# Attention mixing and a 16-expert feed-forward layer on one core: keys later, each expert's down projection at the end of its own slot, one shared chunk in halves

## The reference, cut to what matters

```python
xn = layernorm(x)                                   # x: 2 x 1024 tokens of 256
# attention part (a linear form, no softmax)
Xn = layernorm(xn, gamma, beta)
Q, K, V = split(Xn @ W_in + b_in, 3)
K, V = rotary(K), rotary(V)
A = sum over tokens of unit(K) * unit(V)            # one row of 256 per batch
A = 0.5 * A + 0.5
attn = (A[:, None, :] * Q) @ W_out + b_out + xn
# feed-forward part
scores = softmax(xn @ gate_w.T);  topk of 4 out of 16 experts, weights renormalised
for each expert e, at most 128 tokens (in order):
    y[tokens] += (silu(xg @ w_gate[e]) * (xg @ w_up[e])) @ w_down[e] * weight
shared = (silu(xn @ sw_gate) * (xn @ sw_up)) @ sw_down      # inner width 352
out = x + attn + y + shared
```

## Time and profile before

| | |
|---|---|
| median of 3 runs | 172.38 us (170.6 to 172.52) |
| the profiled execution | 171.0 us, span 169.2 us |
| TensorE busy | 152.4 us, 90% of the span |
| VectorE, ScalarE, GpSimd busy | 64%, 44%, 58% |
| mean granted TensorE clock | 0.983 |

### The profile page before, as it was taken

How to read it: one execution, slowest core, us unless ns; L and a number is a source line. 1 busy time by engine, 2 the same in 40 slices (tenths; PEclk the granted TensorE clock), 3 DMA queues, 4 the chain that set the end, 5 groups by cost and what they waited for, 6 DMA issues and landing times.

```text
span 169.2 us, 3124 instructions
## 1 busy us (share of the span) xinstructions
PE 152.4 (90%) x1005; PEld 134.3 (79%) x1005; DVE 108.7 (64%) x317; ACT 74.6 (44%) x227; POOL 98.1 (58%) x127
## 2 busy tenths in 40 slices
PE   7987797999998999999989999999899999999450
PEld 5556676999886889988779988978898987999340
DVE  1887998587863387799695769638942225920680
ACT  3034437676467984557483543633422354100000
POOL 8675699782237318897653995576523333306930
PEclk9999999999999999999999999999999999999967
DMA  5999969691014657486557487593832222378067
GB/s 151 344 369 338 568 223 346 202 284 28 2 16 114 196 150 187 133 198 140 153 108 188 133 192 142 126 205 128 190 37 31 35 31 31 31 215 280 5 236 260
DMA packets 25507, 28.53 MB, mean 169 GB/s; under 512 B 4114, under 2 KB 24563, under 8 KB 25460
## 3 DMA queue, kind: packets, MB, share of 16 engines
q1 hardware_dynamic: 21042, 22.90, 43.1%
q0 software_dynamic: 3072, 4.33, 15.5%
q10 hardware_dynamic: 1378, 1.12, 2.1%
HBM read 21.64 MB, written 8.79 MB: 180 GB/s over the span
## 4 chain that ended last, share of the span: by engine, by line
DMA 38%; issue 16%; POOL 15%; DVE 13%; PE 11%; ACT 2%; POOLq 1%; DVEq 1%; SPq 0%
DMA ysum<-eo,idx 32%; POOL xg L426 6%; POOL ysum L434 3%; DMA x_all<-ysum 3%; PE bank L247 3%; DVE st L671 3%; POOL xn_all L465 3%; PE bank L249 2%; PE bank L248 2%; DMA x_all<-in_x 2%; DVE xn_all L980 1%; POOL wqt L416 1%; DMA rows<-wd 1%; DVE xt_all L701 1%; DVE mv L674 1%
## 5 line engine op out<-in xcount | busy, mean ns | idle before, releaser
L434 POOL DMA_INDIRECT ysum<-eo,idx x16 | 31.6, 1975 | 33.4 <-DMA ysum<-eo,idx 22.2
L247 PE MATMUL bank<-wkvr_s,xt_all 128*128 128x256 f32 (+1 forms) x96 | 29.9, 311 | 6.9 <-DVE xt_all L701 3.7
L248 PE MATMUL bank<-wkvr_s,xt_all 128*128 128x256 f32 (+1 forms) x96 | 27.7, 288 | 0.0
L249 PE MATMUL bank<-wkvr_s,xt_all 128*128 128x256 f32 (+1 forms) x96 | 27.6, 288 | 0.0
L247 PEld LDWEIGHTS bank<-wkvr_s,xt_all 128*128 128x128 f32 x96 | 18.6, 194 | 8.5 <-DVE xt_all L701 4.7
L1173 PE MATMUL bank<-xgt,wgu 128*128 128x128 f32 (+1 forms) x192 | 24.0, 275 | 0.0
L1173 PEld LDWEIGHTS bank<-xgt,wgu 128*128 128x128 f32 (+1 forms) x192 | 22.4, 187 | 0.1
L426 POOL DMA_INDIRECT xg<-rows,idx x16 | 17.3, 1084 | 8.4 <-issue 4.0
L247 PE MATMUL bank<-xt_all,sw_s 128*128 128x512 f32 (+1 forms) x48 | 21.0, 438 | 0.0
L248 PE MATMUL bank<-xt_all,sw_s 128*128 128x512 f32 (+1 forms) x48 | 18.9, 394 | 0.0
L249 PE MATMUL bank<-xt_all,sw_s 128*128 128x512 f32 (+1 forms) x48 | 18.9, 393 | 0.0
(11 more groups left out here) (167 smaller groups left out, 352.5 us busy)
## 6 DMA issues: line engine op xcount, KB each, us to landing
wgu<-in_w_gu SPq DMA_DIRECT2D x16, 368.0 KB
rows<-xn_all SPq DMA_DIRECT2D x4, 512.0 KB, 6.8
wdn<-in_w_dn SPq DMA_DIRECT2D x16, 128.0 KB
x_all<-ysum SPq DMA_DIRECT2D x4, 512.0 KB, 7.2
x_all<-in_x SPq DMA_DIRECT2D x3, 512.0 KB, 7.2
trg<-in_trig SPq DMA_DIRECT2D x1, 1024.0 KB, 7.5
out<-xn_all ACTq DMA_DIRECT2D x4, 256.0 KB, 3.7
out<-xn_all SPq DMA_DIRECT2D x4, 256.0 KB, 3.1
```

The lines of the kernel that those rows point to most:

```text
L247: nc.tensor.matmul(dst, lt_hi, r_hi, start=start, stop=False)
L248: nc.tensor.matmul(dst, lt_hi, r_lo, start=False, stop=False)
L249: return nc.tensor.matmul(dst, lt_lo, r_hi, start=False, stop=stop)
L434: nc.gpsimd.indirect_dma_start(out=ysum, out_offset=bass.IndirectOffsetOnAxis(ap=idx[:, e:e + 1], axis=0), in_=eo[:, e % G, :], in_offset= ...
```

## The change

What it does:

1. Start: TensorE computes keys 0 to 7 in steps 7 to 13 and 15 instead of from step 2. `turn_pair(1)` moves to step 1. On VectorE the statistics of tiles 6 and 7 go ahead of the loop, the K folds to step 4, the K remainder to step 5; the first shared fold to step 9 and its remainder to step 12. The exponentials and `weights` of tiles 8 to 11 are done by themselves at steps 12 and 13, those of 12 to 15 behind the loop. SyncE saves `wd` in three parts instead of two. `query_bias` moves from slot 1 to ahead of the first shared product.
2. GpSimd: `query_weights` moves from behind step 2 to between the first five gathers and the first scatter.
3. Loop, TensorE: `down(e)` goes to the end of slot e, behind its unit. The third chunk of shared group 2 (unit 11) is done in halves in slots 10 and 11. `combine` writes bank 4 instead of 5, and the wait for `acol` stands ahead of the row turn.
4. Loop, ScalarE: `weigh(e - 1)`, `evac(e + 1)`, `shared_hi`, `silu(e)`. VectorE: `shared_lo` ahead of `gated(e)`.
5. Mixing: both halves of M in one bank; one `mix_hi` and one `mix_lo` of 512 columns per batch; unit 16 ahead of both `mixing(1, .)`; `mix_lo(1)` behind `mix(0)`.
6. End: `ysum` is added to tiles 12 to 15 by VectorE (one 1024-wide add ahead of `keep` of units 17 and 18) instead of GpSimd.

```diff
-KEY_STEPS = ((), (), (0,), (), (1,), (), (2,), (), (3,), (4,), (), (5,), (6,), (), (), (7,))
+KEY_STEPS = ((), (), (), (), (), (), (), (0,), (1,), (2,), (3,), (4,), (5,), (6,), (), (7,))
-M_BANK = ((6, 7), (4, 0))
+M_BANK = (7, 4)
...
# SyncE
-            sp.wait_ge(wd_done, 1)
-            sp.dma_start(rows_v[:, 2 * G:TILES, D:ROW], wd[:, 2 * G:TILES, :]).then_inc(wd_saved, 16)
+            for g in (2, 3):
+                sp.wait_ge(wd_done, g - 1)
+                sp.dma_start(rows_v[:, g * G:g * G + G, D:ROW], wd[:, g * G:g * G + G, :]).then_inc(wd_saved, 16)
...
# GpSimd
             for e in range(XG - 1):
                 gather(e)
+            query_weights()
             for e in range(E):
...
-                if e == 2:
-                    query_weights()
...
-            for t in range(2 * G, TILES):
+            for t in range(2 * G, 3 * G):
                 add_y(t)
...
# ScalarE, the start
             for t in range(TILES):
                 keep_values(t)
-                if t == 0:
+                if t == 1:
+                    hi_pair(1)
+                elif t and t % 2 == 0 and t // 2 + 1 < TILES // 2:
+                    hi_pair(t // 2 + 1)
+                if t == 5:
                     weights_hi(2, slice(0, DC), slice(VR, VRK), 5)
...
-                if t == 5:
+                if t == 10:
                     shared_weights_hi(0)
                 if t == 9:
-                    exps(0, 2 * G, 0)
+                    exps(0, 2 * G)
+                if t == 12:
+                    exps(2 * G, 3 * G)
...
-            exps(2 * G, TILES, 1)
+            exps(3 * G, TILES)
...
# ScalarE, the loop
+                if e:
+                    weigh(e - 1)
                 if e + 1 < E:
                     evac(e + 1)
-                if e == 12:
-                    mix_hi(0, 0)
-                silu(e)
                 if q is not None:
                     shared_hi(q)
+                silu(e)
                 if e == 12:
-                    mix_hi(0, 1)
-                if e:
-                    weigh(e - 1)
+                    mix_hi(0)
...
# VectorE, the start
             stats(4, 6)
-            dve.wait_ge(kq_in, 16)
-            dve.wait_ge(sv_done, 4)
-            fold(1, slice(VR, VRK), bank[4])
-            dve.wait_ge(sv_done, 5)
-            fold(0, slice(VR, VRK), bank[5])
+            stats(6, 8)
             for t in range(TILES):
...
-                if t == 0:
+                if t in (0, 2):
+                    stats(8 + t, 10 + t)
+                if t == 3:
+                    dve.wait_ge(cst_in, 32)
+                if t == 4:
+                    dve.wait_ge(kq_in, 16)
+                    dve.wait_ge(sv_done, 5)
+                    fold(1, slice(VR, VRK), bank[4])
+                    fold(0, slice(VR, VRK), bank[5])
+                    stats(12, 14)
+                if t == 5:
+                    stats(14, 16)
                     dve.wait_ge(whi_done, 3)
                     nc.vector.tensor_tensor(wkvr_s[:, :, 1, VR:VRK], wf[:, :, VR:VRK], f(wkvr_s[:, :, 0, VR:VRK]), ALU.subtract).then_inc(klo_done, 1)
-                if t == 3:
-                    dve.wait_ge(cst_in, 32)
-                if t < 5:
-                    stats(6 + 2 * t, 8 + 2 * t)
-                if t == 4:
+                if t == 9:
                     shared_fold(0)
-                if t == 7:
+                if t == 12:
                     shared_rest(0)
+                if t == 13:
+                    weights(2 * G, 3 * G)
...
-            weights(2 * G, TILES)
+            weights(3 * G, TILES)
...
+            query_bias()
...
# VectorE, the loop
-                gated(e)
                 if q is not None:
                     shared_lo(q)
+                gated(e)
                 if e == 12:
-                    mix_lo(0, 1)
+                    add_bout(0)
+                    mix_lo(0)
                 if e in SUMS:
                     sums(SUMS[e])
-                if e == 1:
-                    query_bias()
...
# VectorE, the end
             shared_lo(11)
-            for t in range(2 * G):
+            mix(0)
+            mix_lo(1)
+            for t in range(1, 2 * G):
                 mix(t)
-
-            for n in (17, 18):
-                dve.wait_ge(ot_pool, G + 2 * (n - 16))
-                keep(n)
+            add_y(3)
+            dve.wait_ge(ot_dve, 1)
+            keep(17)
+            keep(18)
             mix(2 * G)
             mix(2 * G + 1)
-            dve.wait_ge(y_in[0], 16)
             dve.wait_ge(half_done, G)
-            nc.vector.tensor_tensor(sh[:, 0:G, :], sh[:, 0:G, :], yin[:, 0:G, :], ALU.add).then_inc(ot_dve, 1)
+            add_y(0)
...
# TensorE, the start
                 values(t)
-                if t == 0:
+                if t == 1:
+                    turn_pair(1)
                     pe.wait_ge(kq_in, 16)
...
# TensorE, the loop
+                if e - 1 in SUMS:
+                    pe.wait_ge(acol_done, 2 * SUMS[e - 1] + 2)
                 if e + 1 < E:
                     turn_rows(e + 1)
                 if e:
                     gate_up(e)
                 if e in SUMS:
                     reduce_tokens(SUMS[e], e)
-                if e - 1 in SUMS:
-                    pe.wait_ge(acol_done, 2 * SUMS[e - 1] + 2)
-                if e:
-                    down(e - 1)
-
-                if e == 12:
+                if e == 14:
                     pe.wait_ge(m_lo, 1)
-                if e == 14:
-                    pe.wait_ge(m_lo, 2)
...
-                if FILL[e]:
+                if e == 10:
+                    pe.wait_ge(sm_done, 8)
+                    shared_half(8, unit_bank(11), 0)
+                elif e == 11:
+                    shared_half(8, unit_bank(11), 1).then_inc(sh_done, 1)
+                else:
                     unit(e)
                 if e in SUMS:
-                    combine(SUMS[e], e)
+                    combine(SUMS[e])
+                if e < E - 1:
+                    down(e)
...
+            unit(16)
             pe.wait_ge(xgt_done, E)
             mixing(1, 0)
-            unit(16)
-            pe.wait_ge(mid_done, 2 * E)
             mixing(1, 1)
```

More of the change, by code:

```diff
@@ L916, in columns @@
                 dve.wait_ge(comb_done, b + 1)
-                nc.vector.tensor_scalar(acol[:, b, 0:1], bank[5][:, 4:5], 0.5, None, ALU.add).then_inc(acol_done, 1)
+                nc.vector.tensor_scalar(acol[:, b, 0:1], bank[4][:, 4:5], 0.5, None, ALU.add).then_inc(acol_done, 1)
                 nc.vector.tensor_scalar(acol[:, b, 1:2], cs[:, b, 1:2], 0.5, 0.5, ALU.mult, ALU.add).then_inc(acol_done, 1)
@@ L922, in add_bout, with mix_lo @@
                 dve.wait_ge(mix_in, 32)
-                dve.wait_ge(m_done, b * DC + 1)
-                row = bank[M_BANK[b][0]][0:1, 0:D]
+                dve.wait_ge(m_done, b * DC + 2)
+                row = bank[M_BANK[b]][0:1, 0:D]
                 nc.vector.tensor_tensor(row, row, bout_row[:, :], ALU.add).then_inc(mb_done, 1)
-            def mix_lo(b, c):
-                dve.wait_ge(m_hi, b * DC + c + 1)
-                nc.vector.tensor_tensor(m_s[:, b, c, 1, :], bank[M_BANK[b][c]][:, 0:D], f(m_s[:, b, c, 0, :]), ALU.subtract).then_inc(m_lo, 1)
+            def mix_lo(b):
+                dve.wait_ge(m_hi, b + 1)
+                nc.vector.tensor_tensor(m_s[:, b, :, 1, :], bank[M_BANK[b]][:, :].rearrange("p (c n) -> p c n", c=DC), f(m_s[:, b, :, 0, :]),
+                                        ALU.subtract).then_inc(m_lo, 1)
             shared_mid(0, 0)
@@ L947, in _ @@
                     shared_mid(q, unit_bank(e - 1) if e else 2)
+                if q is not None:
+                    shared_lo(q)
+                gated(e)
                 if e == 12:
                     add_bout(0)
-                    mix_lo(0, 0)
-                gated(e)
-                if q is not None:
-                    shared_lo(q)
-                if e == 12:
-                    mix_lo(0, 1)
+                    mix_lo(0)
                 if e in SUMS:
                     sums(SUMS[e])
-                if e == 1:
-                    query_bias()
                 for i in KEYS[e]:
@@ L967, in _ @@
             shared_mid(10, unit_bank(E - 1))
+            shared_lo(10)
+            shared_mid(11, unit_bank(E))
             add_bout(1)
-            shared_lo(10)
-            mix_lo(1, 0)
-            shared_mid(11, unit_bank(E))
             nc.vector.reciprocal(s2[:, :], xn_all[:, :, INV]).then_inc(s2_done, 1)
@@ L1102, in _ @@
                     last_row_and_bias(1, bank[5][:, 0:D], slice(VR, VRK))
-                if t == 2:
-                    keys(0)
-                if t % 2 == 0 and t // 2 + 1 < TILES // 2:
+                if t and t % 2 == 0 and t // 2 + 1 < TILES // 2:
                     turn_pair(t // 2 + 1)
-                for i in KEY_STEPS[t] if t != 2 else ():
+                for i in KEY_STEPS[t]:
                     keys(i)
```

54 lines of the change are left out of this document (25 added, 29 removed).

## The result

The changed kernel takes 164.04 us in the median (163.77 to 164.25), the kernel before beside it 172.45: the ratio is 0.954, 95% interval 0.947 to 0.960. The forecast was 166.0, with a range of 162.7 to 169.6. The profiled execution took 164.1 us with a span of 162.3. The kernel before took between 168.53 and 174.51 us in the 37 runs made beside this and the later kernels, so the 8.4 us between the medians is uncertain by some us; the fastest runs of the two lie 4.8 us apart (168.53 and 163.77).

The account below looks back on a forecast made before the run. GpSimd's scatter chain bounds, TensorE close behind and then the bound. TensorE's terms (-0.7 +1.3 +0.4 -2.2 +0.4) put the last mix at 158.4, span 163.4, execution 165.2; forecast 166.0 us, range 162.7 to 169.6.

Parts of the forecast that it names:

- Rival B: GpSimd's scatters stay the bound, half of the query-weights gain lost to slow issues: 167.8 to 169.5 us, chance 0.24.
- Part 1, the start: Keys later and statistics earlier, before the expert loop: first gather and whole loop move by -0.7 us, bounds 0 and -2.9.
- The sign named for being wrong: At the start of the expert loop: the forecast is wrong if the first gather moves by more than 2 us.
- rival C: Start limited by GpSimd's normalisation, not VectorE: -2.9 us instead of -0.7, time 163.0, chance 0.14.
- Part 2, `down`: Down projection in its own expert slot on TensorE: +1.3 in slot 0, +0.4 in small waits, -2.2 us removed.
- Slot 0: TensorE at down(0) waits for `mid`, since ScalarE is behind by its squares and shared work goes first: +1.3 us.
- The removed waits of the first shared-down slots: Slots 1, 6 and 12 on TensorE: `down` in between gives the low halves time, -2.2 us of 2.5.
- Part 3, mixing: Fifth and sixth mixed tile on TensorE reuse banks VectorE frees later: +0.4 us, bounds 0 and +1.5.
- Part 4, the scatters: GpSimd's scatter chain: first scatter at 61.7 (-1.0 us), last at 138.8 instead of 143.96, leaving the chain runner-up to TensorE.
- The step with the query weights: GpSimd's 9.16 us step between two scatters becomes 5.0 us (-4.2) with the query weights in earlier idle time.
- The end: TensorE's last matmul of mixed tile 13 at 156.5, VectorE's last mix at 158.4 instead of 164.16, then 5.0 us of output.
- The rule against adds on VectorE: VectorE's two-SBUF-input adds and GpSimd's adds exclude each other; all serial they end at 157.1, before 158.4: sum unchanged.

Follow-up runs that it names:

- slot 0 mended: The changed kernel with silu(0) and gated(0) ahead of shared_hi and shared_lo, and the squares of the first four key tiles behind them: 162.77 us.
- the run with slot 0 mended and `down` back: The changed kernel with down(e-1) behind the next gate/up and its old order, and ScalarE's first four squares behind silu(0): 163.60 us.

## Why the prediction was right

**The bound.** Said: the chain of scatters is the bound and TensorE close behind, so the gain ends where TensorE begins. So it was: with the halves undone the time followed TensorE (1.2 us) and not the last scatter (2.0), with `down` undone the last scatter came 4.7 us later at almost no cost, and giving four adds back to GpSimd moved nothing. The start and slot 0 moved the time by their full size, but they move both engines. Rival B, that the scatters stay the bound, is what the runs with the query weights back and the one with the query weights alone show, not this kernel. The number fared less well than the mechanism: it is inside the range because several terms were off in opposite directions, as the parts show.

**Part 1, the start: -0.7 said, about -2.0 measured.** This is the term that was mis-sized most. The working gave VectorE's low half ahead of `values(8)` at 25.6; it ran at 24.61, and `values(8)` began at 25.35 instead of 27.83, 2.5 us earlier. I took 1.42 back for two key tiles. They do come later, but the routing chain doesn't pay for them: the indices were computed at 45.71 instead of 47.34, 1.6 us earlier. The smaller last save of `wd`, which I had put off the path, gave 0.43 more, since the gather waits for its landing. The sign named for being wrong (a first gather moved by more than 2 us) was met to the hundredth; rival C's bound of -2.9 wasn't reached.

**Part 2, `down`.** Slot 0: +1.3 said. The wait was 1.18, but from the second row turn of slot 0 (54.39) to slot 1 it is 5.32 us, where 3.00 as before and 0.68 for `down` were to be expected, so slot 0 cost TensorE 1.6, and its cure gave the time 1.27. No waits in the slots behind: right. The removed waits of the first shared-down slots: slot 12 lost all of its 1.15, slot 1 0.45, slot 6 (4.69 against 5.43) 0.74, together 2.3 where I had -2.2. With the order put back, these three slots last 5.09, 5.13 and 5.98 us, 2.3 longer again, so it was `down` that removed them (the list of waits gives only 1.7 of it). For slots 10 and 11 with the halves and the wait for `acol` I had +0.4; no wait is listed there, but slots 9 to 11 last 16.45 us instead of 16.07 (16.07 again with the order put back), +0.4. As a whole that is 2.3 removed and 2.0 added, and the time moved by 0.2; with slot 0 mended the move earned 0.8. My terms had -2.2, +1.3 and +0.4.

**Part 3, mixing: +0.4 said, +0.8 in the trace.** TensorE's first matmul of mixed tile 0 and its first of unit 17, before and after:
```profile
143.05 0.47 PE L247 MATMUL bank<-wkvr_s,xt_all 128*128 128x256 f32 x1
...
148.85 0.28 PE L247 MATMUL bank<-swd_s,smid_s 128*128 128x256 f32 x1
```
```profile
140.74 0.47 PE L247 MATMUL bank<-wkvr_s,xt_all 128*128 128x256 f32 x1
...
147.34 0.27 PE L247 MATMUL bank<-swd_s,smid_s 128*128 128x256 f32 x1
```
The eight mixed tiles take 6.60 us instead of 5.80. One wait of 0.24 us is listed there (at 144.16, for a mix of VectorE); the pause round it costs 0.4 us, one at 145.14 another 0.2, and the rest is a slightly slower pace. These are mixed tiles 4 and 5, whose banks VectorE frees with `mix(0)`, behind `shared_lo(11)`, and with `mix(1)`, behind `mix_lo(1)`. No run of its own took the mixing back, so that its new bank and order are the cause stays argued.

**Part 4, the scatters.** First scatter 61.7 said, 60.66 measured. The step with the query weights: 5.0 said, 5.31 measured, but not by the step's own cure: the query weights alone left it at 7.33. I put the whole of 4.2 us on them, and half of it hung on a scatter issue of 3.40 us that went away with the new place of `down`. "The other steps I copy, since they are bound by landing" failed in the good direction: the last scatter came at 136.80 and not 138.8, 1.0 by the start and 1.3 by the other steps, less the 0.3 above. The copy kept the long issues of the kernel before: its sixteen scatters took 31.6 us to issue, those of the changed kernel 26.5. That undoing the step costs some 4 to 5 us in the changed kernel is shown (4.2 and 5.3); that it gives as much alone is not.

**The end.** Last mix at 158.4 said, 158.02 measured, but by errors that nearly cancel. TensorE's last matmul of mixed tile 13 started at 155.74 where the sum had 156.5: the start gave 1.3 more than said, slot 0 took 0.3 more and the mixing 0.4 more, and small ones make up the rest. Behind it the sum forgot the length of the last matmul (0.28): from the start of that of tile 15 to the end of the last mix it is 0.87 us, where I had 0.5. From the last mix to the end of the span I copied 5.0 us; it took 4.3. And I said 166.0 for a sum of 165.2, to meet a median above the profiled execution; here the median lies 0.1 under it. So the forecast is too high by 0.4 + 0.7 + 0.9 = 2.0 us.

**The rule against adds on VectorE.** It holds, and changed nothing, as said: see below.

## What to carry to other kernels

Where an engine issues a serial chain of transfers, look at what else is queued between two of them: 3 us of preparation put back between two scatters of the changed kernel cost 4 to 5 there and nothing in a gap ahead of the chain, and such a delay isn't made up when a link takes as long as the work that feeds it. A long step of a chain may have two causes at once: here the one in plain sight, the queued preparation, was half of it. When a bound moves over to another engine, edits on the old one's side are worth their slack and nothing more; test each by itself, since one of them (here the wait in slot 0) may give back what another brings. Where an undone piece makes a wait appear, find in the timeline which instruction waits before you name its cause.

## What the runs showed of the hardware that I had not expected

**VectorE and GpSimd.** In the changed kernel a 96x256 remainder took 1.91 us beside the query weights (VectorE, then GpSimd):
```profile
52.89 1.91 DVE L780 TENSOR_TENSOR swd_s<-aw,swd_s 96x256 fp32r<-96x256 f32 x1
...
53.22 1.29 POOL L417 TENSOR_TENSOR wqt<-wqt,eo 128x512 f32<-128x512 f32 x1
```
It ends at 54.80, just after GpSimd's, which ends at 54.51. With slot 0 mended, the same two instructions miss each other:
```profile
52.77 0.41 DVE L784 TENSOR_TENSOR swd_s<-aw,swd_s 96x256 fp32r<-96x256 f32 x1
...
53.70 1.28 POOL L417 TENSOR_TENSOR wqt<-wqt,eo 128x512 f32<-128x512 f32 x1
```
VectorE is through at 53.18, before GpSimd starts this one. At the end of the changed kernel, four GpSimd adds take 2.61 us (149.49) with no VectorE add beside them, and 3.60 beside VectorE's 1024-wide add in the run with `down` back, where that one takes 1.73 instead of 1.22 (its rows stand above). The Trainium skill, "SBUF — State Buffer", section "Who interferes with whom", has the two engines share a port pair under an exclusive lock; by that, the trace agrees. That a small instruction can pay a whole one of the other engine was known from the Trainium skill, but I had costed it only at the end, where it cost nothing.

**Long issues on GpSimd.** Some issues of an indirect transfer took 2.8 us or more where most take 1.0 to 1.6 (67.54 and 98.00 above, 67.89 in the earlier trace rows). There are 23 in the expert loops of the thirteen traces, and each lies beside 2.0 us or more of VectorE instructions that read both inputs from SBUF (products, accumulations, rotations and the shared part's low halves); no issue within 0.15 us of the usual length has more than 1.75 us of them beside it. The plainest case is no transfer at all, a product of 128x4 on GpSimd in the run with slot 0 mended and `down` back, which takes 0.2 us elsewhere (GpSimd, then VectorE):
```profile
90.23 2.69 POOL L442 TENSOR_TENSOR wprod<-nrm 128x4 f32<-128x4 f32 x1
...
90.37 0.28 DVE L894 TENSOR_TENSOR home_b<-x_all,vr_all 128x128 f32<-128x128 f32 x1
...
92.11 0.75 DVE L903 TENSOR_TENSOR home_b<-home_b,trg 128x256 f32<-128x256 f32 x2
```
It ends at 92.92, when VectorE's row of such instructions ends (92.86). In the four kernels with `down` in its old place this falls on the second scatter (3.37 to 3.49 us), in the nine others on the gather behind it (2.57 to 3.08), during which the scatter before is landing anyway: that is how the place of `down` came to shorten a step of GpSimd. It is a reading of the traces; no run moved these VectorE instructions by themselves to test it.

**The scatter of the times.** The kernel before ran between 168.5 and 174.5 us in 37 runs, and the three with query weights back between 167.1 and 170.7. The changed kernel and those near it stay within about 0.4 us of their median but for three single runs (0.9 to 1.3 above). The kernels that vary are those whose last scatter is issued at 142.6 us or later; what varies in them no run tells.
